# The two GAT layers' products taken by halves of the nodes, in a four-layer graph kernel

## The reference

```
x = _layernorm(x + L0(adj, x))   # max over up to 25 neighbours, then a dense layer, relu
x = _layernorm(x + L1(x, adj))   # GAT: softmax of leaky_relu(s1[i] + s2[j]) where adj, times z, elu
x = _layernorm(x + L2(x, adj))   # GAT with other weights
x = _layernorm(x + L3(x, adj))   # masked attention, two steps with tanh

# L1 and L2
e = leaky_relu(s1[:, :, None] + s2[:, None, :], 0.2)
attention = softmax(where(adj > 0, e, -9e15), axis=-1)
h_prime = attention @ z
return elu(h_prime)
```

## Time and profile before

| | before |
|---|---|
| median of 3 runs | 2069.22 us (2068.86 to 2071.86) |
| profiled execution | 2056.89 us, span 2055.2 us |
| PE busy / PEld busy | 1570.2 us / 1179.2 us |
| DVE busy | 1439.9 us |
| POOL busy | 1358.2 us |
| ACT busy | 680.9 us |
| mean granted TensorE clock | 0.877 |

### The profile page before, as it was taken

The page is one execution under the profiler, slowest core; times in us unless marked ns, Lnnn a source line. Parts: engine busy times, 40 slices in busy tenths (PEclk is TensorE's granted clock), DMA queues, the critical chain, the costliest instruction groups (busy, mean ns, idle before and its releaser), DMA issues.

```text
span 2055.2 us, 28031 instructions
## 1 busy us (share of the span) xinstructions
PE 1570.2 (76%) x9086; PEld 1179.2 (57%) x9086; DVE 1439.9 (70%) x3518; ACT 680.9 (33%) x1372; POOL 1358.2 (66%) x1358
## 2 busy tenths in 40 slices
PE   4666678796778787796788887796788887695777
PEld 3444466474665576474665666464665666474645
DVE  6645688776886688767876688767876788745531
ACT  4011123523244323533244323533244322522252
POOL 5753477777777776777777777777777777771000
PEclk9888978898899978998889988998889978997899
DMA  4111122423233322333224322333224321311010
GB/s 149 40 54 48 50 70 73 123 82 93 71 90 114 112 72 68 111 93 92 71 71 133 95 90 71 109 92 92 71 70 133 105 78 51 110 53 45 1 62 11
DMA packets 79675, 165.44 MB, mean 81 GB/s; under 512 B 24477, under 2 KB 41770, under 8 KB 79530
## 3 DMA queue, kind: packets, MB, share of 16 engines
q0 software_dynamic: 42752, 87.64, 15.7%
q1 hardware_dynamic: 36778, 75.98, 11.2%
HBM read 159.33 MB, written 4.19 MB: 80 GB/s over the span
## 4 chain that ended last, share of the span: by engine, by line
PE 31%; DVE 27%; POOL 14%; DVEq 10%; issue 9%; ACT 7%; DMA 1%; POOLq 0%; ACTq 0%
POOL gathered L426 13%; PE spare L689 9%; DVEq L65 7%; PE big L775 5%; DVE pooled L1024 4%; DVE probs_t L1128 4%; PE side L872 3%; DVE keys L962 3%; PE big L856 3%; DVE hot L1053 2%; PE big L846 2%; DVEq L967 1%; PE big L889 1%; PE big L822 1%; ACT adj_t L457 1%
## 5 line engine op out<-in xcount | busy, mean ns | idle before, releaser
L426 POOL DMA_INDIRECT gathered<-in_x_dram,rows x1336 | 1354.6, 1014 | 502.7 <-issue 432.5
L689 PE MATMUL spare<-hot,x_part 128*128 128x512 f32 x1056 | 313.1, 457 | 53.0 <-DVE best_t L1064 43.8
L1024 DVE TENSOR_REDUCE pooled<-gathered 128x128 f32<-128x2816 f32 (+1 forms) x64 | 304.0, 4749 | 40.3 <-DMA gathered<-in_x_dram,rows 38.1
L689 PEld LDWEIGHTS spare<-hot,x_part 128*128 128x128 f32 x1056 | 233.3, 227 | 117.8 <-DVE best_t L1064 51.4
L775 PE MATMUL big<-values,probs_t 128*128 128x129 f32 x2048 | 246.2, 283 | 0.0
L775 PEld LDWEIGHTS big<-values,probs_t 128*128 128x128 f32 x2048 | 243.1, 199 | 4.9
L1053 DVE TENSOR_SCALAR hot<-running 128x2048 fp32r<-128x2048 bf16 x132 | 159.2, 1233 | 82.0 <-PE spare L689 64.7
L1128 DVE SCALAR_TENSOR_TENSOR probs_t<-row_gain,col_gain,adj_t 128x1024 f32<-128x1024 f32 x128 | 158.0, 1304 | 22.9 <-ACT row_gain L508 22.9
L1175 DVE TENSOR_REDUCE neg_max<-big 128x1 f32<-128x1024 f32 x64 | 77.7, 1222 | 125.2 <-PE big L859 124.7
L856 PE MATMUL big<-xt,row_gain 128*128 128x512 f32 x256 | 134.4, 651 | 34.3 <-ACT adj_less L451 20.0
L872 PEld LDWEIGHTS side<-recip_diag,work 128*128 128x128 f32 x1024 | 128.3, 201 | 52.9 <-issue 43.2
(11 more groups left out here) (169 smaller groups left out, 2289.2 us busy)
## 6 DMA issues: line engine op xcount, KB each, us to landing
adj_in<-in_adj_dram SPq DMA_DIRECT2D x128, 512.0 KB, 3.6
gathered<-in_x_dram,rows POOLq DMA_INDIRECT x1336
xs<-in_x_dram SPq DMA_DIRECT2D x8, 512.0 KB, 4.2
out_dram<-xs SPq DMA_DIRECT2D x8, 512.0 KB, 3.3
w_sb<-in_L_gnn_W_dram SPq DMA_DIRECT2D x1, 128.0 KB
w_sb<-in_L_gnn_W_dram SPq DMA_DIRECT2D x2, 64.0 KB
probs_t<-in_L_gnn_W_dram SPq DMA_DIRECT2D x1, 64.0 KB
gat_w<-in_L_gnn_W_dram SPq DMA_DIRECT2D x1, 64.0 KB
```

Source lines behind the costliest of these rows:

```text
L426: rows_gathered[t % RING].raised_by(pool.indirect_dma_start(out=gathered[:, t % RING, k * C:(k + 1) * C], out_offset=None, in_=x_rows, in_ ...
L689: last = nc.tensor.matmul(spare[:, :], x_parts[part][:, m, :], hot[c][:, j, :], start=(m == 0 and part == 0), stop=(m == T - 1 and part == ...
L1024: link(nc.vector.tensor_reduce(pooled[:, t, :], gathered[:, t % RING, 0:n * C].rearrange("p (k c) -> p c k", k=n), AX.X, ALU.max))
```

## The change

In both GAT layers PE now takes tiles 0 to 3 of nodes through all eight j, and then tiles 4 to 7. The wait for `z_ready` moves ahead of the first L770 product, and waits for `gat_probs` stand in the first half alone. In layer 2 one count follows each j of the second half. On DVE the first half's two reciprocals now stand ahead of the side work (`take_heads(0)`), the first half's sum and statistics behind it (`add_heads(0)`), and then the second half's two reciprocals and its sum. On ACT the eight `take_count` copies move between the two halves of the ELU.

```diff
@@ ACT, gat
-                if layer == 2 and exists(b, 1, B, in_loop):
-                    for j in range(T):
-                        take_count(b + 1, 1, j)
-
                 for t in range(T):
+                    if layer == 2 and t == HALF and exists(b, 1, B, in_loop):
+                        for j in range(T):
+                            take_count(b + 1, 1, j)
@@ PE, gat
-                for t in range(T):
-                    if t == HALF:
+                for h in range(2):
+                    tiles = range(HALF * h, HALF * h + HALF)
+                    if h == 0:
                         pe.wait_ge(z_ready.sem, z_ready.at(b, layer))
-                    nc.tensor.matmul(heads[:, t, 0:C + 1], iso_row[:, t * P:(t + 1) * P], value_sum[:, :],
-                                     start=(t % 2 == 0), stop=False, skip_group_check=True)
-                for j in range(T):
-                    pe.wait_ge(gat_probs.sem, gat_probs.at(b, l * T + j + 1))
-                    for t in range(T):
-                        last = nc.tensor.matmul(heads[:, t, 0:C + 1], probs_t[:, j, t * P:(t + 1) * P],
-                                                values[:, j, :], start=False, stop=(j == T - 1),
-                                                skip_group_check=True)
-                        if j == T - 1 and t % 2 == 1:
-                            gat_heads.raised_by(last)
-                    if layer == 2 and j >= HALF and exists(b, 1, B, in_loop):
-                        if j == HALF:
-                            spare_maxed(b + 1, 2)
-                        for k in range(2 * (j - HALF), 2 * (j - HALF) + 2):
-                            count(b + 1, 1 - slot, 1, k)
+                    for t in tiles:
+                        nc.tensor.matmul(heads[:, t, 0:C + 1], iso_row[:, t * P:(t + 1) * P], value_sum[:, :],
+                                         start=(t % 2 == 0), stop=False, skip_group_check=True)
+                    for j in range(T):
+                        if h == 0:
+                            pe.wait_ge(gat_probs.sem, gat_probs.at(b, l * T + j + 1))
+                        for t in tiles:
+                            last = nc.tensor.matmul(heads[:, t, 0:C + 1], probs_t[:, j, t * P:(t + 1) * P],
+                                                    values[:, j, :], start=False, stop=(j == T - 1),
+                                                    skip_group_check=True)
+                            if j == T - 1 and t % 2 == 1:
+                                gat_heads.raised_by(last)
+                        if layer == 2 and h == 1 and exists(b, 1, B, in_loop):
+                            if j == 0:
+                                spare_maxed(b + 1, 2)
+                            count(b + 1, 1 - slot, 1, j)
@@ DVE, gat
-                side_work(b, slot, f"gat {layer} heads", in_loop)
-                for t in range(0, T, 2):
-                    dve.wait_ge(gat_heads.sem, gat_heads.at(b, (l * T + t) // 2 + 1))
-                    gat_recip.raised_by(nc.vector.reciprocal(recip[:, t:t + 2], heads[:, t:t + 2, C]))
-                if picks and layer == 2:
-                    make_hot(b + 1, 3)
-                for h in range(2):
+
+                def take_heads(h):
+                    for t in range(HALF * h, HALF * h + HALF, 2):
+                        dve.wait_ge(gat_heads.sem, gat_heads.at(b, (l * T + t) // 2 + 1))
+                        gat_recip.raised_by(nc.vector.reciprocal(recip[:, t:t + 2], heads[:, t:t + 2, C]))
+
+                def add_heads(h):
                     tiles = slice(4 * h, 4 * h + 4)
...
+                take_heads(0)
+                side_work(b, slot, f"gat {layer} heads", in_loop)
+                add_heads(0)
+                take_heads(1)
+                if picks and layer == 2:
+                    make_hot(b + 1, 3)
+                add_heads(1)
                 layer_norm(slot)
```

## The result

The changed kernel takes 2071.33 us in the median of 20 runs (2064.09 to 2076.51), the kernel before 2064.18 us in the median of 20 (2053.16 to 2071.86). The ratio is 1.0034, with a 95% interval from 1.0019 to 1.0049: the change is slower, by 7 us where 17 were forecast. The profiled executions differ by 10.8 us (2067.69 against 2056.89). A third of the 15.2 us between 2086.5 and 2071.33 comes from the level: the forecast stood on the median of three runs, 2069.22 us, and the median of 20 is 5.0 us lower.

The account below looks back on a forecast made before the run. POOL's gather chain was taken as the bound, through `pool_tile` 1's release for tile 4. Terms of 0.65, 0.4 and 2.15 us, 3.2 a graph, gave +17.3 us after slack and last-graph gain: 2086.5 us, range 2075 to 2100.

Parts of the forecast that it names:

- the level: Whole kernel: timed median 12.33 us above the profiled execution's 2056.89 us, so the same difference was put on the forecast.
- the bound below: Whole kernel, if all six graphs went the short way from tile 7 to tile 1: +6.4 us, 2075.6 us.
- the sum: Whole kernel: 18.1 us of later tile 1 releases after slack, less 0.8 us in the last graph, +17.3 us.
- term 1: Layer 1, ahead of the side work: DVE waits for the first half's products and takes the second reciprocal, 0.65 us.
- the slack: Tile 4's gather: delay absorbed before POOL waits, 4.2 us in graph 0, 0.5 in graph 1, 0.6 in graph 6.
- term 2: Layer 1, after the side work: ACT's ELU of eight tiles ends later, 4.6 us after that point instead of 4.2, 0.4 us.
- term 3: Layer 2, ahead of `find_keys` and `pool_tile` 1: DVE waits for the first half's products and reciprocal, 2.15 us.
- Layer 2, the tail: Layer 2, behind `pool_tile` 1: second sum ends 4.1 us earlier, worth nothing because DVE already waits at tile 7.
- The last graph: Graph without side work: first half's sum runs under the products, gaining 0.4 us a layer, 0.8 us.
- the tail that would make the kernel faster: Graph ends set by DVE's and PE's own work, so the earlier tail gains: -22.2 us, 2047; chance 0.08.
- the wait that would stay hidden: Tile 4 has at least 3.2 us of slack in timed runs, nothing changes: 2066 to 2072 us; chance 0.07.
- Rival 3: PE's longer idle at graph ends puts more of layer 0 at the lower clock: 2098 to 2104 us; chance 0.10.

Follow-up runs that it names:

- e11: The kernel before with 2.4 us more DVE work ahead of the side work in layer 2's heads: ratio 1.0097 to the kernel before.
- e12: The kernel before with the same 2.4 us of DVE work behind layer 2's side work, ahead of the four reciprocals: ratio 1.0007 to the kernel before.
- e5: The changed kernel with tile 1's reduction ahead of the first half's reciprocals, the search for keys behind them: 2052.00 us against 2062.86, ratio 0.9957 to the kernel before.
- e13: The kernel before with tile 1's reduction ahead of the search for keys in layer 2, nothing else: ratio 0.9973 to the kernel before.
- e10: The changed kernel run again, unaltered, for a second trace and comparison: ratio 1.0058 to the kernel before.
- e4: The kernel before with 2.4 us more DVE work ahead of layer 2's side work, run where the kernel before took 3153.22 us: ratio 1.0029.

## Why the prediction was right in its direction and wrong in its size

**The bound** was read rightly. POOL's chain of gathers sets the end of each graph, and the release of tile 1 is its only narrow place: e11 and e12 show it by dose, e5 and e13 by taking the wait away.

**What failed** are sizes. The level failed, the 12.33 us put on top of the profile: it came out 5.0 us too high. With 2064.18 us in its place the same sum gives 2081.5, and the bound below, +6.4 us, gives 2070.6, just under the measured 2071.33. And the sum failed, +17.3 us where the traces show 10.9 and the timed runs 7. In the sum it was above all the landing of the gathered rows, which the prediction put at nothing when it called the earlier tail worth nothing, and then layer 1's wait (term 1) and the slack. Each follows with its number.

**Layer 1, the wait (term 1, 0.65 us)** failed as a mechanism in most graphs. "The first half is 4 + 32 products from 981.82, done at 990.9" took the rate of its products, 0.253 us, from graph 3 of the trace before. There the granted clock was 0.79 in the mean over the first 8 us of the products. In five of the seven graphs it was 1.00 over the same stretch, and the same 64 products took less, as in graph 2:

```profile
754.34 14.56 PE L775 MATMUL big<-values,probs_t 128*128 128x129 f32 x128
```

That is 0.2275 us each. Graph 1 in the second trace of the changed kernel (e10) has PE where the prediction put it, its first row 4.2 us after the start of the probabilities (520.73), and still no wait:

```profile
516.56 9.91 DVE L1129 SCALAR_TENSOR_TENSOR probs_t<-row_gain,col_gain,adj_t 128x1024 f32<-128x1024 f32 x8 [1.43 <-ACT row_gain L508]
...
521.81 7.41 PE L777 MATMUL big<-values,probs_t 128*128 128x129 f32 x64
...
529.51 0.23 DVE L1140 RECIPROCAL recip<-big 128x2 f32<-128x2 f32 x2
```

The granted clock was 1.00, and the first half is complete at 529.2, 0.3 us ahead of DVE. PE's start varies besides. In graph 3 of the trace before, the pick and the start of the probabilities stood side by side:

```profile
977.63 4.91 DVE L1128 SCALAR_TENSOR_TENSOR probs_t<-row_gain,col_gain,adj_t 128x1024 f32<-128x1024 f32 x4 [1.43 <-ACT row_gain L508]
977.71 4.18 PE L689 MATMUL spare<-hot,x_part 128*128 128x512 f32 x16
```

In the changed kernel the pick starts 1.3 us ahead of the probabilities:

```profile
982.06 3.89 PE L688 MATMUL spare<-hot,x_part 128*128 128x512 f32 x16
983.36 3.68 DVE L1129 SCALAR_TENSOR_TENSOR probs_t<-row_gain,col_gain,adj_t 128x1024 f32<-128x1024 f32 x3 [1.44 <-ACT row_gain L508]
```

Over the two picks the granted clock was 0.93 and 1.00, and PE's first product comes 3.6 us after the start of the probabilities instead of 6.2. In both traces of the changed kernel five of seven graphs have no wait there. The other two, in which PE's first row comes 5.4 or 5.5 us after the start of the probabilities, wait 0.8 us, and their side work begins 1.1 us later. With the two reciprocals' own time, the side work begins 0.4 us later in the mean over the seven graphs.

**Layer 1, the tail (term 2, 0.4 us)** held. ACT's copy starts 4.4 us after the side work in the four traces with layer 1 by halves, and 4.1 in the others, 0.3 us. By these rows layer 1 costs 0.7 us a graph where 1.05 were forecast. How much of it reaches layer 2 is less certain: from the start of layer 1's probabilities to that of layer 2's, the mean of graphs 1 to 6 over the six traces with layer 1 in the old order is 51.5 us (51.1 to 51.9), and over the four by halves 52.1 (51.6 to 52.3), 0.5 us.

**Layer 2, the wait (term 3, 2.15 us)** has the right mechanism and the right mean, and the mean in part by luck. From the start of the probabilities to the release the means of before are 22.3 in both traces, those of the changed kernel 24.8 and 24.3, and that of layer 2 alone 24.6: 2.2 us. But the term used the slow 0.253 us a product once more, and graph 3's early start of PE, 3.5 us after the probabilities, where five of the seven graphs of that trace have 4.3 to 4.8. The two errors offset each other. In the four graphs of e10 in which PE did start at 3.4 to 3.6 us the release comes 1.5 us later, and where it started at 4.4 to 4.6 in the two traces, 2.4 to 2.7 us later.

**The three terms together** came out well. From tile 7's reduction to tile 1's last row the means over graphs 1 to 6 are 114.0 and 113.4 us before and 116.7 in both traces of the changed kernel, 3.0 us a graph where 3.2 were forecast: 2.2 in layer 2, 0.5 in layer 1, and 0.3 ahead of layer 1, which is no more than the two traces of before differ by.

**Layer 2, the tail** came 3.9 us earlier where 4.1 were forecast, and was worth nearly nothing, as the prediction said and e12 shows from the other side. It seems not to have been worth exactly nothing, and that was missed. When DVE is ready earlier at the end of a graph, ACT finishes the normalization earlier too, and the graph's 512 KB store and the next load are issued earlier. At the end of graph 6 the store, the last gather and the reduction stood so, before:

```profile
1856.55 0.40 SPq L365 DMA_DIRECT2D out_dram<-xs  x1
...
1861.46 0.94 POOL L426 DMA_INDIRECT gathered<-in_x_dram,rows  x1 [0.30 <-issue]
...
1865.35 4.86 DVE L1024 TENSOR_REDUCE pooled<-gathered 128x128 f32<-128x2816 f32 x1 [8.71 <-DMA gathered<-in_x_dram,rows]
```

and so in the changed kernel:

```profile
1865.87 0.40 SPq L365 DMA_DIRECT2D out_dram<-xs  x1
...
1873.94 0.94 POOL L426 DMA_INDIRECT gathered<-in_x_dram,rows  x1 [0.30 <-issue]
...
1876.47 4.86 DVE L1025 TENSOR_REDUCE pooled<-gathered 128x128 f32<-128x2816 f32 x1 [10.50 <-DMA gathered<-in_x_dram,rows]
```

From the last gather's end to the reduction it was 1865.35 - 1862.40 = 2.95 us and is 1876.47 - 1874.88 = 1.6 us. In the second traces the same end took 4.9 and 1.5 us, so about 2.4 us of the loss come back at that end alone. The six ends ahead of it have 2.2 us in the mean before and 2.0 in the changed kernel, 1.4 us more in six cycles, though two traces of one kernel differ by as much. That the store and the loads are the cause is only argued, from their order in time.

**The slack and the waits.** The slack of graphs 1 and 6 was read rightly from the one trace, 1.1 us. The second trace of before has 2.0 us, in four graphs, and 5.2 us of waits instead of 9.3. POOL's waits rose by 15.0 us where the sum had 18.1. The 3.0 us a graph make 18.1 over six; 1.4 are taken by the shorter landing, 1.6 by the slack, and 0.3 by gathers ahead of tile 4 that took a little longer.

**The last graph** gives 0.5 us (189.7 to 189.2 us behind the stretch, means of two traces each), where 0.8 were forecast.

So the sum should have been about 15 for the waits, less 2.4 for the last landing, less about 1 for gathers that were a little quicker, less 0.5: 11 us. That is what the traces show, 11.4 us more in the stretch and 0.5 less behind it. The timed runs say 7 us, with an interval of 4 to 10, and 12 in the second comparison (7 to 17). What separates 7 from 11 stays open. The traces of one kernel differ by 11 us ahead of the stretch, and that is more than the gap.

Of the rivals, the tail that would make the kernel faster and the wait that would stay hidden didn't happen. Rival 3, more of layer 0 at the lower clock, didn't either: from tile 7's reduction to layer 1's probabilities the means are 40.1 and 39.8 us before and 40.3 and 40.2 after. The rule of the Trainium skill, "Perfetto Trace Analysis", section "Identifying the Most-Contended Engine", would have named DVE. Its busy time is 1458.2 us in e11 and 1460.7 us in e12, and one loses 20 us and the other nothing measurable, so that occupancy didn't find the bound here. POOL was found by its waits.

## What to carry to other kernels

When an engine works for the next piece of data through a small ring of buffers, look for the one instruction that frees a place, and ask what stands ahead of it on its engine. Once the slack is used up, a delay that is put there costs its length in every cycle, and work behind it costs nothing as long as the engine waits for the ring anyway, as 2.4 us of dummy work here showed on either side. If the ring's release can be moved ahead of a wait, do that first: one swapped entry in a table earned 5.6 us in the kernel before, and the same move turned the changed kernel's loss of 7 to 12 us into a gain of 9.

And when a term is the difference of two arrival times (products ready, DVE there), take it over all cycles of the trace and not from one, above all where the clock moves one of the two. And take the level from as many runs as the range is narrow: a median of three stood 5 us above a median of 20 here.

## What the runs showed of the hardware

A matmul stream can be held up within a group, by something that no semaphore shows: in e4, beside a kernel before at 3153 us, PE's products idled 240 us on "issue", mostly one product at a time, while POOL's gathers were as quick as ever (981 ns in the mean, 1014 in the trace of before). I found no cause for it in the profile, whose chain puts 29% of the span to "another core or an unknown queue".

The last gather of graph 6's end lands 1.5 us or up to 4.9 us after POOL has issued it, with the same bytes. In the eight traces with 2.95 us or more a 512 KB store was issued between 4.9 us ahead of that gather and 0.1 us behind its start, with loads right after it; in the three with 1.5 or 1.6 us (the changed kernel twice, layer 2 alone) the store was 7 to 9 us ahead.
